# Three slots instead of two for the one-hot tensors of the edge-count build (a four-layer graph network)

## The reference

```
h = max(layernorm(x), 0)
layer 0:  x += segment_sum(edge_weight * (sigmoid(h @ Wg + bg) * (h @ W))[src], dst)
layer 1:  x += segment_sum(h[src], dst) @ W1.T + b1
layer 2:  messages of (h[src], h[dst]) @ Wm + bm, summed at dst, then [h, agg] @ Wu + bu
layer 3:  hypergraph convolution (sum to edges, weigh, sum back), batch norm, relu
```

## Time and profile before

| | us |
|---|---|
| median of three runs | 2705.81 |
| the profiled execution, its own time | 2705.83 |
| its span, first to last instruction | 2703.9 |
| outside the span | 1.9 |
| TensorE busy | 2359.7 (87%) |
| VectorE busy | 1605.8 (59%) |
| ScalarE busy | 1239.3 (46%) |

### The profile page before, as it was taken

How to read it: one execution, slowest core, us unless ns; L and a number is a source line. 1 busy time by engine, 2 the same in 40 slices (tenths; PEclk the granted TensorE clock), 3 DMA queues, 4 the chain that set the end, 5 groups by cost and what they waited for, 6 DMA issues and landing times. The chain is left out here.

```text
span 2703.9 us, 72658 instructions
## 1 busy us (share of the span) xinstructions
PE 2359.7 (87%) x27976; PEld 2019.8 (75%) x27976; DVE 1605.8 (59%) x3701; ACT 1239.3 (46%) x2693; POOL 37.9 (1%) x46
## 2 busy tenths in 40 slices
PE   3679898998889898988974999899998999999996
PEld 2457777777777776777764888788887888878774
DVE  6679998998989898998964233333343212121114
ACT  2477776777777676777734222223222000011113
POOL 3100000000000000000000000000000000000000
PEclk9689999999999999999987999999999999999997
DMA  6289999999999999999998999989998999999994
GB/s 186 66 155 195 199 204 195 188 201 178 196 178 203 194 183 199 180 208 180 201 185 209 277 276 275 280 230 250 255 254 224 289 290 290 271 235 249 248 252 116
DMA packets 1745895, 584.13 MB, mean 216 GB/s; under 512 B 1258166, under 2 KB 1742394, under 8 KB 1745511
## 3 DMA queue, kind: packets, MB, share of 16 engines
q1 hardware_dynamic: 1742379, 572.41, 100.7%
q0 software_dynamic: 1600, 4.92, 0.6%
q10 hardware_dynamic: 1660, 3.20, 0.5%
HBM read 255.26 MB, written 89.20 MB: 127 GB/s over the span
## 5 line engine op out<-in xcount | busy, mean ns | idle before, releaser
L1155 ACT CAST stage<-ps 128x784 f16<-128x784 f32 x784 | 655.0, 835 | 134.9 <-DMA counts_by_source<-stage 96.1
L611 PE MATMUL ps<-Ha,a_pairs 128*128 128x258 f16 x4802 | 548.6, 274 | 47.0 <-ACT Ha L1200 39.2
L611 PEld LDWEIGHTS ps<-Ha,a_pairs 128*128 128x128 f16 x4802 | 470.2, 98 | 117.2 <-ACT Ha L1200 39.4
L564 PE MATMUL ps<-hot_c,hot_r 128*128 128x98 f16 x3136 | 513.4, 213 | 11.2 <-DVE hot_c L862 5.9
L565 PE MATMUL ps<-hot_c,hot_r 128*128 128x98 f16 x3136 | 507.6, 211 | 6.5 <-issue 6.5
L566 PE MATMUL ps<-hot_c,hot_r 128*128 128x98 f16 x3136 | 506.5, 211 | 0.0
L1138 ACT CAST stage<-ps 128x392 f16<-128x392 f32 x784 | 397.6, 507 | 200.6 <-PE ps L547 200.6
L539 PE MATMUL ps<-g_in,wt 128*128 128x128 f16 x2401 | 438.9, 225 | 43.3 <-DVE X L874 31.3
L540 PE MATMUL ps<-g_in,wt 128*128 128x128 f16 x2401 | 435.8, 223 | 0.0
L541 PE MATMUL ps<-g_in,wt 128*128 128x128 f16 x2401 | 435.2, 223 | 0.0
L874 DVE SCALAR_TENSOR_TENSOR X<-ps,X 128x512 f32<-128x512 f32 (+1 forms) x637 | 391.9, 653 | 17.0 <-PE ps L541 17.0
(11 more groups left out here) (198 smaller groups left out, 2106.7 us busy)
## 6 DMA issues: line engine op xcount, KB each, us to landing
a_pairs<-counts_by_source SPq DMA_DIRECT2D x75, 3136.0 KB, 14.1
counts_by_source<-stage SPq DMA_DIRECT2D x50, 1568.0 KB, 9.3
gated_parts<-G SPq DMA_DIRECT2D x7, 448.0 KB, 3.0
g_in<-gated_parts SPq DMA_DIRECT2D x98, 32.0 KB, 3.3
out_x<-X SPq DMA_DIRECT2D x6, 512.0 KB
edge_table<-tab SPq DMA_DIRECT2D x1, 2448.0 KB, 9.6
wt<-stage SPq DMA_TRANSPOSE x98, 10.9
a_turned<-counts_by_source SPq DMA_TRANSPOSE x49, 8.8
```

The costliest lines, as they stand in the source:

```text
L564: mm(into(0), rows_, codes(0), start=v == 0, stop=True, skip_group_check=True)
L611: last = mm(ps[:, c % 2, 0:PARTS], a_slot(ph, c, i), moving[:, i], start=i == 0, stop=i == TILES - 1)
L1155: a.copy(stage[:, b, 0:2, :, u * SET_COLS:(u + 1) * SET_COLS], of).then_inc(s("hi_done"), 1)
```

## The change

`hot_r` and `hot_c` get three slots in place of two. A round's slot is its running number modulo 3, where it was its parity (8 rounds in a tile, so the slot of a round differs from tile to tile; the loop of six tiles has 48 rounds, a multiple of 3). VectorE's wait before codes(h) lets it start when the round three before is done by TensorE, where it was the round two before. The two tensors grow by 2,048 and 4,704 bytes in each partition, so `stage`, `wt` and `g_in` move up by 6,752 bytes, and `dst_run` of the preamble moves from behind `G` to a place below.

```
+HOT_SLOTS = 3
...
+def hot_at(c, h):
+    return (c * TILE_HOTS + h) % HOT_SLOTS
...
-        hot_r, o = at("hot_r", [P, 2, PAIRS, P, 2], F16, o)
-        hot_c, o = at("hot_c", [P, 2, PAIRS, 1 + WEIGHTS, WCOLS, 2], F16, o)
+        hot_r, o = at("hot_r", [P, HOT_SLOTS, PAIRS, P, 2], F16, o)
+        hot_c, o = at("hot_c", [P, HOT_SLOTS, PAIRS, 1 + WEIGHTS, WCOLS, 2], F16, o)
...
+        dst_run, r = at("dst_run", [P, RUN + 1], I32, r)
         assert r <= wt_at, (r, wt_at)
         G, o = at("G", [P, TILES, 2, P], F16, wt_at)
-        dst_run, o = at("dst_run", [P, RUN + 1], I32, o)
...
-                    h, bank = (u // 2) % 2, 2 * unit_at(c, u)
+                    h, bank = hot_at(c, u // 2), 2 * unit_at(c, u)
...
-                def hots(j, h):
-                    b = h % 2
+                def hots(j, c, h):
+                    b = hot_at(c, h)
                     hot = j * TILE_HOTS + h
-                    if not (isinstance(j, int) and j == 0 and h < 2):
-                        dve.wait_ge(s("unit_done"), hot * 2 - 2)
+                    if not (isinstance(j, int) and j == 0 and h < HOT_SLOTS):
+                        dve.wait_ge(s("unit_done"), (hot - HOT_SLOTS + 1) * 2)
...
-                        hots(j, h)
+                        hots(j, c, h)
```

## The result

The changed kernel takes 2682.45 us (median of four runs, 2680.57 to 2683.85) against 2708.31 us for the kernel before beside it: a ratio of 0.990, 95% interval 0.988 to 0.992. The forecast was 2681, which is 24.3 us under the 2705.8 that it started from; the measured fall is 25.9 us. The profiled execution has a span of 2680.4 us in place of 2703.9. (Lines behind the inserted code are six higher: L859 is now L865, L874 is L880, L1155 is L1161, L547 is L553, L541 is L547. In the experiments they move by a few more.)

The account below looks back on a forecast made before the run. VectorE's beat, slowed by stalls of the two-tile ring through `stage` and by loop jumps, bounds the build. 18.7 us from 17 stalls plus 7.2 from six jumps, less 1.6 for the clock, takes 2705.8 to 2681 us; range 2658 to 2703.

Parts of the forecast that it names:

- tiles 1 to 12: Build before the first jump back: five stalled tiles on the path (2, 4, 6, 9, 11) each save 1.1 us.
- jumps back: Six loop jumps in the build: codes(4) start 1.2 us earlier at each, 7.2 us together; VectorE's 4.22 us instruction wait stays.
- 12 further stalls x 1.1, less 1.6 for the clock: Two stalls per later six-tile group save 1.1 us each; two more path tiles dropping to a lower clock return 1.6.
- 17 fills: ScalarE's restart to the tile's hand-on, 17 of 31 stalls on the path: each shrinks 1.1 us, from 22.05 to about 20.95.
- 17 chains: Hand-on's start to ScalarE's restart two tiles later, 26.4 us at tile 25: length unchanged, costed at nothing.
- rival B: Hand-on chain grows by what the fill shrinks, so only jumps back gain: 2698.6 us, no measurable change; chance 0.15.
- A path that has another number of stalls: Sign of being wrong: the path setting the build's end has a stall count other than the forecast 17.
- The next wait: VectorE's codes wait falls from 102.8 to some 60 us or less; adds wait for sums 20 or more; sum 25 smaller.
- The clock: TensorE's clock drops in long stalls, 0.8 us more per tile; two more path tiles fall into it, costing 1.6 us.
- That the hand-on's chain keeps its length: Hand-on to store's release in `stage`: length kept if each tile on a ring moves by the same amount; zero cost.
- Rivals C, D and E: C: change inert or register instruction shows, 2706 or 2696 (0.05); D: moved transposes slower, 2726 (0.08); E: store faster, 2647 (0.05).
- Rival A: Each stall and jump back on the path yields a full codes block, 1.97 us: 45 us, time 2661; chance 0.12.

Follow-up runs that it names:

- experiment 1: Changed kernel with three slots and moved tensors kept, but VectorE again waiting for the round two before: 2708.65 us, against 2708.17 for the kernel before.
- the four three-slot loop kernels: Changed kernel profiled twice, and twice with 160 bytes free ahead of `stage` (its old address phase): builds 1207.8, 1215.6, 1218.4 and 1207.8 us.
- the two with the old wait: The kernel before, and the changed kernel with VectorE waiting for the round two before: builds 1233.1 and 1234.5 us.
- Experiments 4 to 7: Build's 49 tiles written out without jumps back, each form run twice: kernel before (two slots) 2671.89 and 2675.11 us, changed kernel (three) 2658.4 and 2652.88.
- written-out kernels: Kernels before and after with the build's 49 tiles written out on four engines: ratios 0.989 and 0.988 (two slots), 0.983 and 0.982 (three).
- the first pair: First runs of the kernels before and after with the build written out: 2671.89 us with two slots, 2658.4 with three.
- experiments 8 and 9: Kernels before and after with each tile's store issued from ScalarE's queue beside the transposes: 2760.26 us (two slots) and 2759.01 (three).
- experiments 1 to 3: Changed kernel with the old wait value, 2708.65 us; then twice with 160 bytes free ahead of `stage`, 2690.23 us and, beside its partner, ratio 0.992.
- experiment 8: Kernel before (two slots) with each tile's store issued from ScalarE's queue beside the transposes: 2760.26 us, ratio 1.021.

## Why the prediction was right

*The total* was right for the reason given, which experiment 1 isolates. By its terms, with the mean of the four three-slot loop kernels against that of the two with the old wait:

| term | forecast | measured |
|---|---|---|
| tiles 1 to 12 (5 stalls x 1.1) | -5.5 | 304.3 to 302.1: -2.2 |
| jumps back (6 x 1.2) | -7.2 | 188.7 to 181.4: -7.3 |
| 12 further stalls x 1.1, less 1.6 for the clock | -11.6 | 740.9 to 729.0: -11.9 |
| build | -24.3 | 1233.8 to 1212.4: -21.4 |

The first twelve tiles gave less than half of what I put there, and their profiles scatter between 297 and 304 us. That the other two terms agree to 0.3 us is luck in part: with the wait kept the jump tiles took 186.4 and 190.9 us, and with three slots the other thirty took 723.1 to 732.2.

*The agreement of the total hides errors that cancel.* The path can be followed back in the two profiles of the result, from the last hand-on to ScalarE's restart, to the hand-on two tiles before, and so on. It goes through 17 stalls in both, as forecast. Its parts, in us:

| part of the path | forecast | before to after |
|---|---|---|
| 17 fills | -17.1 | 385.6 to 362.5: -23.1 |
| 17 chains | 0 | 476.1 to 479.1: +3.0 |
| six jump tiles | -7.2 | 186.4 to 181.5: -4.9 |
| eight undisturbed tiles | 0 | 185.0 to 184.8: -0.2 |

A fill on the path lost 1.4 us and not 1.1, and the chains took 3 us back; in the first twelve tiles the five fills lost 5.8 us and the five chains gained 4.4. So the small gain there is the forecast's rival B at work in this profile. In the other three profiles with three slots the path has 18, 20 and 18 stalls (17 with the old wait), fills of 21.5 to 22.0 us on average where two slots have 22.6 and 22.7, and chains of 28.1 to 28.3 where two slots have 27.9 and 28.0. "A path that has another number of stalls" was a sign of being wrong; it shows in three of four, and the total holds in spite of it.

*The next wait* was named rightly (the adds wait for the sums), but its size was not: I expected some 60 us to stay at the codes and 20 or more at the adds. Nearly all of it moved: 1.4 and 81.0 us. The sum of both fell by 37 us and not by 25, because 12.7 us more of VectorE's idle time is booked to missing instructions. The forecast's own steps say so, since codes that start up to 2 us earlier leave no stall long enough to be seen at L865.

*The clock* cost more, and the fill gained more, than in the sum. At full clock a fill shrinks by 1.25 us (20.80), in place of 1.1; 17 of the 32 fills behind a wait for the store (tile 3 on) last 21.2 us or less in the kernel after; the others are at 21.4 to 22.9. Over all fills the mean went from 22.4 to 21.4 us, so the 1.1 that I put for a stall was near the mean of both. The forecast also laid the drop to long stalls. That does not hold: ScalarE had waited 3.12 us in tile 27 of the kernel before, where the clock stayed at full, and 3.09 us in tile 15 of the kernel after, where it fell to half.

*The jumps back* were given to VectorE's 4.22 us. The term came out, but its account was one-sided. TensorE stands still for its own instructions at the same places, and for longer, as this row of its timeline in the kernel after shows:

```profile
613.82 0.50 PE L553 MATMUL ps<-stage,minus 128*128 128x392 f16 x1 [6.88 <-issue]
```

Six such waits are 39.9 us, and (181.5 - 6 x 23.1) = 42.9 us is what the jump tiles cost above the beat. In the kernel before TensorE has one such wait, of 6.9 us; at the other jumps its time was booked to VectorE's codes, which were late as well (waits of up to 7.1 us). Experiments 4 to 7 take both away: 188.7 to 151.3 us for the six tiles with two slots.

*That the hand-on's chain keeps its length* (rival B is the contrary) held in the loop kernels: the mean from a hand-on's start to ScalarE's restart was 27.3 and 27.6 us with the old wait and 27.5 to 28.1 with three slots. A little was given back, not all. In the written-out kernels three slots gave 18 us where a fixed chain would give 29. There fills shrank by 0.8 us on average (22.3 to 21.5): only 13 and 14 of some 43 came down to 21.3 us or less, the rest follow stalls shorter than 1.5 us, which leave less to win, or long ones that mostly end with the clock at half. And the chain was 0.7 us longer in the first pair and equal in the second (27.05 to 27.75, 27.43 to 27.38). The lower fill gain is shown; how much the chain takes back from run to run is left open, and so is whether it can take back all: in experiments 8 and 9 the third slot gave 1 us by the medians, but 13 us in the profiles' builds.

*Rivals C, D and E* fell with experiments 1 to 3. *Rival A* fell by the trace: behind the stall of tile 16 the adds still wait. *Rival B* is right in small part, as the chains of the path show.

## What to carry to other kernels

A further buffer pays only where its wait ends last, and only up to the next wait in the same engine's program order: work out the second one before counting the first. Where a stall comes from elsewhere (here a ring of two tiles through `stage` and the DMA engines), a buffer shortens the recovery behind it, so its price is gained once per stall on the path that sets the end, not once per stall in the table of waits. And a loop's jump back can cost more than the change under study: written out, the same kernel is 24 to 36 us faster.

## What the runs showed of the hardware

- In the kernel after, a jump back over six tiles of code costs TensorE 6.4 to 7.0 us without instructions, and VectorE 3.9 to 4.3 us, then 1.5 to 2.5 us more a few instructions later (the two "issue" rows of the kernel after). The Trainium skill (Runtime: NRT & Kernel Launch, "Instruction fetch mechanics") says that a taken branch out of the fetched window stalls; the trace agrees and gives the size, and written out the build has no such wait (experiments 4 to 7).
- A transpose and a store gain nothing side by side on two queues here. In the kernel before, the DMA engines move 217 GB/s under a transpose alone (848 to 853 us) and 283 under a store alone (842 to 846); with both under way in experiment 8 (822 to 834) they move 195. The issue of the transpose takes 16.1 us, and the kernel is 2.1% slower.
- After nearly equal idle times of TensorE in two stalls (the first row is the kernel before, the second the kernel after) the granted clock stayed at full in the one and fell to 0.50 (the 1.2 GHz level) in the other. Which of the two a stall gets is worth 1.1 us here, and I could not tell it beforehand.

```profile
824.51 0.34 PE L547 MATMUL ps<-stage,minus 128*128 128x392 f16 x1 [1.85 <-ACT stage L1155]
```

```profile
516.31 0.34 PE L553 MATMUL ps<-stage,minus 128*128 128x392 f16 x1 [1.83 <-ACT stage L1161]
```
